# The transformer block's software pipeline: next groups' norms begun in the last slots, final rows turned beside the next heads, key copies on GpSimd, other slots for scan and softmax

## The reference

```python
h = h + attn_ref(layernorm(h))      # selective scan, forward input plus flipped input, 16 states per channel
h = h + ffn_ref(layernorm(h))
# attn_ref: delta = softplus(x Wd), deltaA = exp(delta*A), dBu = delta*Bf*x + delta_b*Bb*flip(x),
#           scan over tokens, y = sum_n h_n*C_n + x*D + flip(x)*D, y @ Wout.T
# ffn_ref:  rmsnorm, 4-head causal attention with rotary positions, residual,
#           rmsnorm, router over 8 experts (top 2), out = sum_e weight_e * (silu(x w1)*(x w3)) w2
```

## Time and profile before

| | us |
|---|---|
| median of 3 runs (7879.69 to 7908.85) | 7898.49 |
| the profiled execution's own time | 7906.27 |
| its span | 7904.4 |
| attention centre of w = 0 to that of w = 15, per interval (6228.4 to 7752.5, 15 intervals, the first without experts) | 101.6 |

### The profile page before, as it was taken

One profiled execution on the slowest core, in us unless ns is written; L12 is line 12 of the kernel. 1 busy time (PEld: TensorE's weight loads), 2 busy tenths in 40 slices (PEclk: granted clock), 3 DMA queues, 4 the chain that ended last, 5 costly groups with the idle time before them and its releaser, 6 DMA issues. The chain is left out here.

```text
span 7904.4 us, 141712 instructions
## 1 busy us (share of the span) xinstructions
PE 6788.2 (86%) x45682; PEld 4620.4 (58%) x45682; DVE 4865.3 (62%) x7585; ACT 5032.1 (64%) x8721; POOL 4262.9 (54%) x1540
## 2 busy tenths in 40 slices
PE   7888789999799999799998899999999477777777
PEld 4555577777677777577776544444444255444555
DVE  7888657777467777477776333333333566777774
ACT  7888567778477777477777477777777233333332
POOL 7888457777267777177776144444444433333330
PEclk9999899999899999899999999999999687788888
DMA  2222344444444444444444411111111322333330
GB/s 84 94 98 94 129 157 158 159 158 155 162 144 159 154 156 156 153 155 158 152 159 138 140 50 45 49 50 44 50 47 41 99 67 68 69 69 69 69 68 3
DMA packets 597044, 835.29 MB, mean 106 GB/s; under 512 B 451944, under 2 KB 493032, under 8 KB 531304
## 3 DMA queue, kind: packets, MB, share of 16 engines
q1 hardware_dynamic: 596968, 834.27, 33.9%
HBM read 477.54 MB, written 356.58 MB: 106 GB/s over the span
## 5 line engine op out<-in xcount | busy, mean ns | idle before, releaser
L859 POOL TENSOR_TENSOR sb_rstd<-sb_var,sb_minus_half 128x16 f32<-128x16 f32 x1280 | 3690.0, 2900 | 2440.3 <-DVE sb_var L591 1219.3
L598 DVE TENSOR_TENSOR sb_unit<-H,sb_rstd 128x512 f32<-128x512 f32 x768 | 527.3, 687 | 517.1 <-POOL sb_rstd L859 511.7
L555 ACT ACTIVATE sb_pix<-sb_unit 128x512 f32<-128x512 f32 x768 | 827.7, 1078 | 0.0
L505 PEld LDWEIGHTS M<-sb_table,sb_pix 128*128 128x128 f32 x6144 | 712.1, 194 | 144.3 <-ACT sb_pix L555 125.1
L478 PE MATMUL H<-sb_conv_block,sb_act_in 128*128 128x128 f32 x6144 | 777.7, 280 | 0.0
L551 ACT ACTIVATE sb_act_px<-sb_unit 128x512 f32<-128x512 f32 x768 | 485.9, 633 | 451.0 <-DVE sb_unit L604 450.9
L478 PEld LDWEIGHTS H<-sb_conv_block,sb_act_in 128*128 128x128 f32 x6144 | 724.3, 194 | 38.2 <-issue 23.9
L505 PE MATMUL M<-sb_table,sb_pix 128*128 128x52 f32 x6144 | 737.0, 279 | 0.0
L591 DVE TENSOR_REDUCE sb_var<-sb_square 128x16 f32<-128x528 f32 x768 | 502.5, 696 | 236.4 <-ACT sb_square L544 236.4
L822 DVE COPY sb_act_out<-TC 128x512 f32<-128x512 f32 x256 | 177.0, 691 | 644.3 <-PE TC L672 644.3
L1812 ACT ACTIVATE blk_silu<-bank 114x260 f32<-114x260 f32 x384 | 148.7, 387 | 638.4 <-PE bank L1598 635.8
(11 more groups left out here) (273 smaller groups left out, 13588.2 us busy)
## 6 DMA issues: line engine op xcount, KB each, us to landing
act_scratch<-sb_act_out SPq DMA_DIRECT2D x256, 1024.0 KB, 3.9
sb_act_in<-act_scratch SPq DMA_DIRECT2D x256, 1024.0 KB, 5.3
spectrum_in<-sb_f_sb SPq DMA_DIRECT2D x512, 78.0 KB, 1.8
sb_x_in<-spectrum_in SPq DMA_DIRECT2D x48, 832.0 KB, 4.3
spectrum_out<-sb_y_sb SPq DMA_DIRECT2D x48, 832.0 KB, 4.6
sb_z_in<-spectrum_out SPq DMA_DIRECT2D x512, 78.0 KB, 5.1
blk_rows_b<-scan_rows SPq DMA_DIRECT2D x128, 260.0 KB, 7.2
blk_rows_bb<-scan_rows SPq DMA_DIRECT2D x128, 260.0 KB, 8.2
```

Source lines behind the costliest of these rows:

```text
L505: mm = e.matmul(M[u][:, 52 * g:52 * g + 52], pix[1 - p][:, at:at + 128], const("f1"), start=True, stop=True)
L555: e.activation(dst, unit[k % 2][:, :].rearrange("p (x c) -> p c x", c=16), gelu).then_inc(pix_ready, 1)
L598: e.tensor_tensor(rows, H[k][:, :].rearrange("p (y c) -> p y c", c=C), rstd[k][:, :].unsqueeze(2).to_broadcast([128, 16, C]), ALU.mult).th ...
L859: e.tensor_tensor(rstd[j][:, :], var[j][:, :], minus_half[:, :], ALU.pow).then_inc(rstd_ready, 1)
```

## The change

1. The norms of the next window's groups begin in the last slots of this window. The scan group's mean (PE) and centre (DVE) stand in slot 23 (`MEAN_AT`), its square and the experts' square (ACT) behind the last silu, the variances (PE) in slot 24, `half_variance` (DVE) in slot 25. The attention group's mean and centre stand in slot 26, its square, variance and half variance behind the slots. `before` does this once ahead of window -1. The banks of these products change (B[3], B[5], B[6]); the router's result goes to B[3].
2. The load of the logarithm's table stands right behind the last silu.
3. The final rows of group w-2 (`features`, `features_turned`, `final`, `store`) are made in the front of window w: ACT copies after the first guess, PE turns after the router, SP stores between two of its spreads. The last group's are made behind all windows.
4. `q_image` and `kx` go from DVE (slot 0) to POOL (behind `dub`, `q_image` after the third rotary step, `kx` after the sixth).
5. Slots: drive 3, 6, 9, 11 -> 3, 5, 7, 9; scan 6, 9, 12, 14 -> 8, 11, 15, 17; read 13, 15, 16, 17 -> 14, 16, 18, 19; skip 6 -> 9; out 15, 17, 18, 19 -> 16, 18, 20, 21; the two softmax products 11 -> 12 and 13; turning of the probabilities from 12 -> 13; wo, x2, h1 21, 22, 23 -> 22, 23, 24.
6. Windows -1 to 2 are written out and the hardware loop runs over 3 to 13 (before: -1 to 1, and 2 to 13).

```diff
-        TURN_AT = 12
-        WO_AT, X2_AT, H1_AT = 21, 22, 23
-        DRIVE_AT = (3, 6, 9, 11)
-        SCAN_AT = (6, 9, 12, 14)
-        READ_AT = (13, 15, 16, 17)
-        SKIP_AT = 6
-        OUT_AT = (15, 17, 18, 19)
+        WEIGHT_AT = (12, 13)
+        TURN_AT = 13
+        WO_AT, X2_AT, H1_AT = 22, 23, 24
+        DRIVE_AT = (3, 5, 7, 9)
+        SCAN_AT = (8, 11, 15, 17)
+        READ_AT = (14, 16, 18, 19)
+        SKIP_AT = 9
+        OUT_AT = (16, 18, 20, 21)
+        MEAN_AT, VARIANCE_AT = 23, 24
...
@@ tensor: the slots
+                if old:
+                    wait(e, "fin", gx - 1)
                 for n in range(SLOTS):
                     if scan:
                         scan_slot(gs, n, ga if attn else None)
                     if attn:
                         attention_slot(ga, n)
+                    if n == MEAN_AT:
+                        means(w + 1, scan1)
+                    if n == VARIANCE_AT:
+                        variances(w + 1, scan1, moe1)
+                    if n == SLOTS - 1:
+                        attention_mean(w + 1, attn1)
                     if moe:
                         expert_slot(gx, n)
+                attention_variance(w + 1, attn1)
...
@@ scalar
                 if moe:
                     guess(moe_n, "x", gx, 1)
+                if old:
+                    features(gx - 1)
                 if attn:
                     guess(attn_n, "a", ga, 1)
                 if scan:
                     guess(scan_n, "s", gs, 1)
+                if old:
+                    if not scan:
+                        e.wait_ge(stored, 16 * (gx - 1))
+                    final(gx - 1)
...
+                        if n == PARTS * NE - 1:
+                            e.preload_act_table_set("natural_log_exp_and_others")
...
+                    if n == MEAN_AT:
+                        scan_square(w + 1, scan1)
+                        moe_square(w + 1, moe1)
+                attention_square(w + 1, attn1)
...
@@ vector: the slots
+                    if n == MEAN_AT:
+                        next_scan(w + 1, scan1)
+                    if n == VARIANCE_AT + 1:
+                        next_halves(w + 1, scan1, moe1)
+                    if n == SLOTS - 1 and attn1:
+                        centre("a", w + 1, cen, h1, 6)
                     if moe:
                         expert_slot(gx, n)
+                if attn1:
+                    half_variance(attn_n, "a", w + 1, 6, EPS, 1)
...
@@ gpsimd, behind du and dub
+                if attn:
+                    wait(e, "rope", ga, 3)
+                    for i in range(2):
+                        e.tensor_tensor(q_image[i][:, :], qf[:, :], const("image")[:, i:i + 1].to_broadcast([128, TOK]),
+                                        ALU.mult).then_inc(sig["q_image"], 1)
+                    wait(e, "rope", ga)
+                    for q in range(Q):
+                        e.tensor_tensor(kx[:, NH * T * q:NH * T * (q + 1)].rearrange("p (h t) -> p h t", t=T),
+                                        kf[:, T * q:T * q + T].unsqueeze(1).to_broadcast([128, NH, T]),
+                                        const("heads").unsqueeze(2).to_broadcast([128, NH, T]), ALU.mult)\
+                            .then_inc(sig["kx"], 1)
...
@@ sync
                     spread(gs, rows_b, 0, 0, b_in)
                     spread(gs, rows_bb, NS, 0, bb_in)
+                    if old:
+                        store(gx - 1)
                     for k in range(1, CHUNKS):
```

More of the change, by code:

```diff
@@ L1525, in spread, with store, window @@
                         .then_inc(done[k], 16)
-            def window(w, scan, attn, moe):
+            def store(g):
+                wait(e, "fin", g)
+                e.dma_start(out_rows[g], fin[:, :].rearrange("t (m d) -> t m d", m=GI)).then_inc(stored, 16)
+            def window(w, scan, attn, moe, *after):
                 gs, gx = w + 1, w - 1
+                old = moe and not (isinstance(gx, int) and gx == 0)
+                if old and not scan:
+                    store(gx - 1)
                 if scan:
@@ L1548, in window @@
                         load(gs + 1)
[L1549 to L1553, removed]
             load(0)
-            step = window
-            windows(e.Fori, step)
+            windows(e.Fori, lambda *at: None, window)
+            store(groups - 1)
             e.wait_ge(stored, 16 * groups)
@@ L1741, in square, with scan_square, moe_square, attention_square @@
                 e.activation(c.sqr[:, :], src[:, :], ACT.Square).then_inc(done, 1)
-            def window(w, scan, attn, moe):
+            def scan_square(w, scan):
+                if scan:
+                    wait(e, "s_cen", w + 1)
+                    square(scan_n, h_cen, sig["s_square"])
+            def moe_square(w, moe):
+                if moe:
+                    wait(e, "x2", w - 1)
+                    square(moe_n, x2, sig["x_square"])
+            def attention_square(w, attn):
+                if attn:
+                    wait(e, "a_cen", w)
+                    square(attn_n, cen, sig["a_square"])
+            def features(g):
+                wait(e, "down", g)
+                e.activation(feat[:, :], B[4][:, 0:TOK], ACT.Copy).then_inc(sig["feat"], 1)
+            def final(g):
+                wait(e, "feat_turned", g)
+                e.activation(fin[:, :], B[4][0:T, :], ACT.Copy).then_inc(sig["fin"], 1)
+            def before(w, scan, attn, moe):
+                scan_square(w, scan)
+            def window(w, scan, attn, moe, scan1, attn1, moe1):
                 gs, ga, gx = w + 1, w, w - 1
+                old = moe and not (isinstance(gx, int) and gx == 0)
                 def guess(c, name, g, nth):
@@ L1821, in window @@
                             e.preload_act_table_set("silu_and_others")
-                if moe:
-                    wait(e, "down", gx)
-                    e.activation(feat[:, :], B[4][:, 0:TOK], ACT.Copy).then_inc(sig["feat"], 1)
-                    wait(e, "feat_turned", gx)
-                    if not scan:
-                        e.wait_ge(stored, 16 * gx)
-                    e.activation(fin[:, :], B[4][0:T, :], ACT.Copy).then_inc(sig["fin"], 1)
-                    e.preload_act_table_set("natural_log_exp_and_others")
-            windows(e.Fori, window)
+                    if n == MEAN_AT:
+                        scan_square(w + 1, scan1)
+                        moe_square(w + 1, moe1)
+                attention_square(w + 1, attn1)
+            windows(e.Fori, before, window)
+            features(groups - 1)
+            e.wait_ge(stored, 16 * (groups - 1))
+            final(groups - 1)
         @block.vector
@@ L1990, in gate_steps @@
                 order = const("order").unsqueeze(1).to_broadcast([T, GI, NE])
[L1991 removed]
+                logits = e8(B[3][0:T, 0:GI * NE])
                 def shifted():
```

150 lines of the change are left out of this document (77 added, 73 removed).

## The result

The changed kernel took 7920.49 us in the median of 20 runs (7897.46 to 7934.15), the kernel before 7896.60 in 20 runs on the same chips (7879.69 to 7913.60). The ratio is 1.0027, 95% interval [1.002, 1.0035]: slower by some 20 us, where 0.1% less was forecast. It is inside the forecast range and inside the half per cent that was called "the same"; the sign was wrong. The profiled execution took 7925.5 us, its span is 7923.7.

What follows compares the result with a forecast made beforehand. No engine was saturated throughout: PE bounded the first slots and slots 15 on, DVE slots 6 to 14. Window terms -0.6 + 2.0 - 4.6 + 1.3 + 1.3 = -0.6, with the ends -10.7 in all, gave median 7888 us, range 7820 to 7945.

Steps and rivals of the forecast that it cites:

- Tail: From the last silu to DVE's first Newton step: 6.98 us falls to 6.4, gain 0.6 a window.
- The last window's tail: Window 16, experts alone: silu's end to first Newton step falls from 7.18 us to 3.9, gain 3.3.
- Removed copies: Front: DVE loses six products, some 4 us of work; gain 0.2, left at 0.
- Loss 2.0: Front: gate steps on DVE wait beside GpSimd's six products, 2.0 us a window lost; bounds 0 and 4.3.
- The lock waits I take as unchanged: Slots 6 to 14: DVE's port waits on GpSimd (the scan's 2.1 us) stay the same, though they could vanish.
- Gain 4.6: Slots 6 to 14, bound by DVE: scans 2 and 3 move to slots 15 and 17, 4.6 us a window gained.
- the clock's 1.3: Slots 12 to 14: PE's nine products at a slower clock, loss 1.3 us a window, a third of 3.9.
- rival B: Faster: DVE wins the lock beside the gate, PE at full clock behind slot 11; 7842 us, chance 0.33.
- rival D: Half PE clock throughout slots 6 to 14, loss 3.9 instead of 1.3 a window; 7924 us, chance 0.12.
- PE gets more behind slot 14: Slots 15 on, bound by PE: one more turn, value product and scan mean, loss 1.3 us a window.
- A: The main forecast for the whole kernel: 7888 us, spreading 7865 to 7930, chance 0.40.
- C: Slower: GpSimd's new products beside the gate cost 1.28 us, not 0.71; 7968 us, decides from 0.93 a product; chance 0.15.

Runs made afterwards that it cites:

- b_pool: The kernel before with only `q_image` and `kx` moved to GpSimd behind `dub`: 7941.23 us, ratio 1.006.
- a_gate: The changed kernel, copies still on GpSimd, with GpSimd's first chunk product waiting for the gate's last step: 7876.30 us, ratio 0.997.
- a_tie: The changed kernel with `q_image` and `kx` back on DVE and GpSimd's chunk products 1 to 3 waiting for DVE's drives: 7820.12 us, ratio 0.9882.
- b_slots: The kernel before with the new slots alone, norms and copies as before: 7863.96 us, ratio 0.9961.
- b_unroll: The kernel before with window 2 written out and the loop over 3 to 13, nothing else: 7914.72 us, ratio 1.000.
- a_both: The changed kernel with two waits: first chunk product behind the gate's last step, chunk products 1 to 3 behind DVE's drives: 7820.61 us, ratio 0.9873.

## Why the prediction was wrong

**Tail: right.** 6.46 in the window shown, 6.43 in the mean (forecast 6.4). The order was as walked; ACT after:

```profile
7040.17 0.39 ACT L1873 ACTIVATE blk_silu<-bank 114x260 f32<-114x260 f32 x1 [1.37 <-PE bank L1607]
7040.57 1.28 ACT L1875 ACT_TABLE_LOAD   x1
7041.86 0.42 ACT L1778 ACTIVATE blk_sn_sqr<-blk_h_cen 128x260 f32<-128x260 f32 x1
```

**The last window's tail: right, the window not.** From the silu's end at 7855.16 to the first Newton step 3.89 us (forecast 3.9, before 7.18). But the window's front grew by 1.0 and its first slots by 1.3 at a clock of 0.63 for 0.74. Windows 15 and 16 with the end took 0.9 less in all, for the 2.3 forecast:

```profile
7859.05 0.43 DVE L1946 TENSOR_TENSOR blk_mn_y<-blk_mn_y,blk_mn_ve 128x260 f32<-128x260 f32 x1 [0.94 <-ACT blk_mn_y L1814]
```

**Removed copies: right.** DVE's six products fewer gave nothing that shows: PE was bound by the gate, not by them.

**"Loss 2.0" for the gate: right mechanism, too small. This is the step that failed.** Measured 3.0 (24.28 to 27.28), and these 1.0 a window are the whole difference between the window forecast (102.9) and the window measured (103.87): over windows 2 to 14, -7.8 was forecast and +5.4 came. The prediction walked the gate's steps against the six products only. The six cost 0.9, less than half of what I took, since each was 0.59 and not 0.71 and the steps waited 0.1 to 0.3 and not 0.3 to 0.5. Not in the walk was the chunk product that GpSimd starts when its rows have landed. It had stood just behind the gate's end; the gate, 1.3 later, ran into it. b_pool and a_gate show its 2.1. The upper bound of 4.3 covered it by luck.

**"The lock waits I take as unchanged": wrong, and hidden in the sum.** The prediction had GpSimd's eight chunk instructions as the same work, only earlier. It did not set them against the new drives one by one. DVE's groups of drives and scans, before and after:

```profile
L1896 DVE TENSOR_TENSOR blk_rows_b<-blk_rows_b,blk_du 128x1040 f32<-128x1040 f32 x64 | 116.1, 1814 | 9.4 <-DMA blk_rows_b<-scan_rows 9.4
L1905 DVE TENSOR_TENSOR_SCAN blk_rows_b<-blk_dA,blk_rows_b 128x1040 f32<-128x1040 f32 x64 | 186.8, 2919 | 6.0 <-POOL blk_rows_b L2115 4.4
```

```profile
L1972 DVE TENSOR_TENSOR blk_rows_b<-blk_rows_b,blk_du 128x1040 f32<-128x1040 f32 x64 | 161.7, 2527 | 13.5 <-DMA blk_rows_b<-scan_rows 13.5
L1981 DVE TENSOR_TENSOR_SCAN blk_rows_b<-blk_dA,blk_rows_b 128x1040 f32<-128x1040 f32 x64 | 174.0, 2719 | 1.6
```

The drives took 45.6 us more and the scans 12.8 less, some 2 us more a window where nothing was put down. The first slots show it: 13.70 after for 11.85 before, at clocks of 0.76 to 0.81 and 0.77. The total of the slots came out as forecast all the same, since the loss behind slot 14 was not paid and slots 6 to 14 gave 0.65 more: two errors that cancelled, by luck. I had named the waits' vanishing as a possibility and put it below the range with 0.06. a_tie shows that keeping GpSimd behind the drives was worth 4.2 us a window.

**"Gain 4.6" with the clock's 1.3, net 3.3: near in size.** The stretch fell by 3.96, but part of this is the drive's wait that moved into the first slots: with the drive ahead, b_slots has 32.5 and not 30.7 here. Read together, slots 0 to 14 fell by 1.95, where 3.3 was forecast. In the window shown the clock of slots 6 to 14 is 0.81, for 0.75 before: neither rival B's full clock nor rival D's 0.5. Where the clock matters is in the first slots, where PE bounds: 0.76 to 0.81 in 12 of 13 windows after, as in most windows before; b_slots, at 0.94, is 1.8 us shorter in slots 0 to 14.

**"PE gets more behind slot 14", loss 1.3: seen in part.** In the mean the stretch changed by -0.1 (1.3 more were forecast), but the mean of before holds windows 2 to 4 with 27.4 to 27.8 us. Over windows 5 to 14 it is 25.4 before and 25.9 after, 0.5 more.

**Windows -1 and 0, taken as 0.** From the block's first DMA to the end the block took 1759.4 us after and 1751.3 before, 8.1 more, where 10.7 less were forecast. Of the 8.1, windows 2 to 14 are 5.4, window 1 is -0.9, the last ones are -0.9, and the start up to the first Newton step of window 1 is 4.4 (155.5 to 159.9). That start isn't clearly the change's: b_unroll, which has windows -1 and 0 as before, has 158.0.

**Rivals.** The result lies inside A's own range (7865 to 7930), close to D's 7924; the half clock in slots 6 to 14, from which D lives, did not come. C's price was wrong (0.59, not over 0.93), yet something in GpSimd's list did make the front 3.0 longer, of the 5.6 from which C decides. Of the rule in the Trainium skill (SBUF — State Buffer, Who interferes with whom) that issue order and not the kind of operation decides who blocks, and for the whole instruction: the rows agree, 2.25 us for a step of 65x8 elements behind GpSimd, 0.17 without it. I used that rule to price the copies and not to ask which pairs would come to stand in which order. The same page says that a DVE instruction with at most one SBUF input, outside the two-port modes, does not contend with GpSimd; this row of DVE after stood beside GpSimd's `pos` (7059.06 to 7060.48), has one input from a bank, and took 0.43 as elsewhere, so it agrees:

```profile
7059.90 0.43 DVE L1960 TENSOR_TENSOR blk_qf<-bank,blk_tables 128x260 f32<-128x260 f32 x1
```

**Open.** The block accounts for 8 us of the profiled difference of 19, and the medians and their ratio say 21 to 24. The rest lies in the tokenizer, where nothing was changed. Its end moves between 6140 and 6179 us over the profiled kernels, without an order by length of program. b_unroll's median speaks against the longer list, though its interval does not exclude it. It wasn't settled.

## What to carry to other kernels

When work moves to an engine's list, what it slows on the other engine arrives later too: walk the slowed chain to its end, against everything that the first engine starts at a time of its own, such as when a DMA lands. Here the moved work cost 0.9, and the meeting that it caused 2.1. When an instruction wins or loses such a meeting, look at the next stretches before calling it a gain or a loss: a drive that won 2.2 us gave all but 0.2 back at the softmax subtraction. A wait that keeps one engine behind the other at each chunk can be worth more than the edit itself, but it makes that engine later, and what it then meets decides: the same wait gained 0.7% in one order of slots and lost 0.4% in the other, where it met the softmax products.

## What the runs showed that I had not expected

- A start that differs by 0.04 or 0.05 us decides which of two instructions takes 2.2 us longer. The drive of slot 5 lost in all 13 windows of the changed kernel, by 0.04 us in seven of them and by 0.2 to 0.6 in the others, and won in 12 of 13 windows of b_slots.
- A GpSimd instruction can be held for longer than one DVE instruction takes: 6.21 us for one that takes 2.38 alone (a_tie, 7038.50).
- TensorE's granted clock in the first slots is worth 1.8 us a window (0.73 against 0.95 in a_gate), and takes a pattern of its own in each kernel: 0.93 or 0.94 in all 13 windows of a_both; before, from window 6 on, 0.77 and 0.93 in turn, 11.84 and 10.0 us; 0.76 to 0.81 in 12 of 13 after; 0.68 to 0.79 in 12 of 13 in a_tie, at the same total time as a_both. The order of drive and product does not decide it: a_gate has the drive behind in every window, and 0.73 and 0.95 in turn. I can't say what does.
